# Block 0 of a two-layer conditioned transformer: the scores of a batch in one go instead of two halves, and its first exponential moved to the end of its tick

## The reference

```
h = ln(x) * (1 + scale1) + shift1                     # modulated by cond_1024
q, k, v = split(h @ Wqkv + bqkv)
x = x + attn(q, k, v) @ Wos + bos                     # block p = 0
h = ln(x) * (1 + scale2) + shift2
x = x + attn(h @ Wq + bq, ctx @ Wk + bk, ctx @ Wv + bv) @ Woc + boc   # block p = 1
x = x + gelu(ln_mod(x) @ W1 + b1) @ W2 + b2           # block p = 2
attn: softmax(q k^T / 4) v, per head, over 128 x 128 scores
```

## Time and profile before

| | |
|---|---|
| median of 3 runs | 4214.8 us (4213.77 to 4216.97) |
| the profiled execution | 4216.5 us, of which its span (first to last instruction) 4214.5 us |
| mean granted TensorE clock | 0.996 |
| busy share of the span | PE 96%, PEld 82%, DVE 68%, ACT 65%, POOL 69% |
| blocks p = 0 and 1 | from some 60 to 1190 us, 32 groups of 4 batches |

### The profile page before, as it was taken

One profiled execution on the slowest core, in us unless ns is written; L12 is line 12 of the kernel. 1 busy time (PEld: TensorE's weight loads), 2 busy tenths in 40 slices (PEclk: granted clock), 3 DMA queues, 4 the chain that ended last, 5 costly groups with the idle time before them and its releaser, 6 DMA issues.

```text
span 4214.5 us, 95758 instructions
## 1 busy us (share of the span) xinstructions
PE 4065.3 (96%) x34870; PEld 3476.2 (82%) x34870; DVE 2854.7 (68%) x6066; ACT 2751.0 (65%) x10788; POOL 2905.9 (69%) x2706
## 2 busy tenths in 40 slices
PE   7999999999999999999999999999999999999999
PEld 6777777777779987888888888888888888888998
DVE  7888888888865556565656565777777767665443
ACT  6999999999953335666666666666666666665333
POOL 5777788888767775666566565666666666666776
PEclk9999999999999999999999999999999999999999
DMA  2110011111111122212121212322222222221110
GB/s 82 32 32 32 32 47 39 42 47 47 53 51 47 60 64 76 81 71 81 70 80 71 81 70 95 105 78 91 80 89 86 82 87 81 88 98 56 41 51 31
DMA packets 230900, 276.64 MB, mean 66 GB/s; under 512 B 38044, under 2 KB 160416, under 8 KB 230432
## 3 DMA queue, kind: packets, MB, share of 16 engines
q1 hardware_dynamic: 230364, 270.51, 18.9%
q10 hardware_dynamic: 68, 0.02, 0.0%
HBM read 85.89 MB, written 50.33 MB: 32 GB/s over the span
## 4 chain that ended last, share of the span: by engine, by line
PE 78%; POOL 7%; DVE 7%; ACT 5%; issue 3%; DMA 0%; ACTq 0%; SPq 0%; DVEq 0%; POOLq 0%
PE BANKS L607 18%; PE BANKS L609 16%; PE BANKS L608 16%; PE BANKS L801 7%; PE BANKS L765 6%; PE BANKS L753 6%; PE BANKS L687 3%; ACT PR L904 3%; POOL PR L1234 2%; POOL Z L1277 2%; PE BANKS L823 2%; DVE WL L1095 1%; POOL HL L1244 1%; DVE PT L1058 1%; POOL X L1291 1%
## 5 line engine op out<-in xcount | busy, mean ns | idle before, releaser
L1234 POOL TENSOR_TENSOR PR<-PR,RL 128x512 f32<-128x512 f32 x1024 | 1070.2, 1050 | 656.0 <-DVE RL L1063 654.7
L920 ACT ACTIVATE PR<-BANKS,NM 128x128 f32<-128x128 f32 x2048 | 730.5, 382 | 441.8 <-DVE NM L1109 437.4
L904 ACT ACTIVATE PR<-BANKS,NM 128x128 f32<-128x128 f32 x2048 | 730.8, 412 | 12.6 <-DVE NM L1050 10.5
L607 PE MATMUL BANKS<-HH,WH 128*128 128x512 f32 x1632 | 688.8, 422 | 8.6 <-DVE SN L1123 4.3
L801 PE MATMUL BANKS<-ID,PR 128*128 128x128 f32 x4096 | 624.1, 275 | 61.7 <-DVE OL L1102 26.0
L1109 DVE TENSOR_REDUCE NM<-BANKS 128x8 f32<-128x1024 f32 x256 | 313.3, 1224 | 487.3 <-PE BANKS L765 487.3
L608 PE MATMUL BANKS<-HL,WH 128*128 128x512 f32 x1632 | 642.3, 394 | 0.0
L609 PE MATMUL BANKS<-HH,WL 128*128 128x512 f32 x1632 | 642.0, 393 | 0.0
L801 PEld LDWEIGHTS BANKS<-ID,PR 128*128 128x128 f32 x4096 | 487.4, 140 | 187.3 <-POOL PR L1234 66.7
L904 ACT ACTIVATION_READ_ACCUMULATOR PR<-BANKS,NM 128x1 f32 x2048 | 516.6, 253 | 0.0
L920 ACT ACTIVATION_READ_ACCUMULATOR PR<-BANKS,NM 128x1 f32 x2048 | 452.7, 221 | 0.0
(11 more groups left out here) (132 smaller groups left out, 10733.8 us busy)
## 6 DMA issues: line engine op xcount, KB each, us to landing
SW<-SN SPq DMA_DIRECT2D x1024, 128.0 KB, 2.1
x_scratch<-X SPq DMA_DIRECT2D x80, 512.0 KB, 3.1
X<-x_scratch SPq DMA_DIRECT2D x80, 512.0 KB, 4.0
CX<-in_ctx SPq DMA_DIRECT2D x32, 384.0 KB, 4.2
X<-in_x SPq DMA_DIRECT2D x16, 512.0 KB, 3.9
out<-X SPq DMA_DIRECT2D x16, 512.0 KB, 2.9
CX<-in_ctx SPq DMA_DIRECT2D x32, 128.0 KB, 4.1
STG<-in_L_xcond_W SPq DMA_DIRECT2D x4, 512.0 KB, 5.2
```

The source lines that it names most:

```text
L607: e.matmul(o, lh, rh, start=first and i == 0, stop=False)
L904: made = e.activation(pr[:, r], bank[:, r], ACT.Exp, bias=nm[:, h:h + 1], accum_out=RL[npr(t)[0]][:, h:h + 1])
L920: made = e.activation(pr[:, r], bank[:, r], ACT.Exp, bias=nm[:, h:h + 1], accum_out=RL[npr(t)[0]][:, h:h + 1])
L1234: e.tensor_tensor(p3, p3, RL[npr(t)[0]][:, :].unsqueeze(2).broadcast_to([128, 4, 128]), ALU.mult).then_inc(s_nrm, 1)
```

## The change

The scores of a batch become one stage in tick 0, all four row groups in turn inside the loop (24 matmuls), waiting for tile 3 of the batch before. Both maxima move to tick 0 too. The exponentials become a function that is called twice in a tick: tiles 1 to 3 where they were, tile 0 behind copies, hf and gelu. (On `s_s0` each batch still counts 2.)

```diff
             for b in range(G):
                 tb = tg + 4 * b
+                at["scores0", tb].append(Batch(p, g, b))
                 for h in range(2):
-                    at["scores0", tb + 2 * h - 2].append(Half(2 * (4 * (NG * p + g) + b) + h, p, g, b, h))
-                    at["max0", tb + 2 * h - 1].append(Half(2 * (4 * (NG * p + g) + b) + h, p, g, b, h))
+                    at["max0", tb].append(Half(2 * (4 * (NG * p + g) + b) + h, p, g, b, h))
...
-                    q.wait_ge(s_exp, 4 * (4 * ga + x.b) + 2 * x.h - 2)
+                    q.wait_ge(s_exp, 4 * (4 * ga + x.b))
                     for c in range(2):
                         for k, (qt, kt) in enumerate(((AH, KBH), (AH, KBL), (AL, KBH))):
-                            for r in (2 * x.h, 2 * x.h + 1):
+                            for r in range(4):
...
-                    made.then_inc(s_s0, 1)
+                    made.then_inc(s_s0, 2)
...
+            def exponentials(tiles):
+                for t in tiles:
+                    q.wait_ge(s_nm0, t.n // 2 + 1)
+                    q.wait_ge(s_t, t.n - NP0 + 1)
+                    q.wait_ge(s_nrm, t.n - NP0 + 1)
...
+                    made.then_inc(s_exp, 1)
...
-                for t in at["exp0", tick]:
...
+                exponentials([t for t in at["exp0", tick] if t.u])
...
+                exponentials([t for t in at["exp0", tick] if not t.u])
```

More of the change, by code:

```diff
@@ L871, in _ @@
                     e.dma_start(CROWB[r + 1:r + 2, 64 * i:64 * i + 64], a[key][128:CD].unsqueeze(0)).then_inc(s_crows, 16)
+            def exponentials(tiles):
[3 more added lines that the diff above has]
+                    q.wait_ge(s_nrm, t.n - NP0 + 1)
+                    bank, pr, nm = PS[t.u], PR[npr(t)[0]], NM0[t.n // 2 % 3][:, 4 * (t.n % 2):4 * (t.n % 2) + 4]
+                    for h in range(4):
+                        r = slice(128 * h, 128 * h + 128)
+                        made = e.activation(pr[:, r], bank[:, r], ACT.Exp, bias=nm[:, h:h + 1], accum_out=RL[npr(t)[0]][:, h:h + 1])
+                    made.then_inc(s_exp, 1)
             for tick in ticks:
```

## The result

The changed kernel takes 4502.6 us (median of 4 runs, 4500.6 to 4504.0) against 4215.9 for the kernel before: a ratio of 1.068, with a 95% interval of 1.067 to 1.069. It is 287 us slower. The prediction was 4513.

A forecast was written before the change was run, and what follows sets the result against it. No single engine but the fixed order of four loaded engines was taken to bound p = 0 and 1. Span 4214.5 + 117 + 86 + 95 = 4512, plus 2.0 outside is 4514.5, so 4513 us for the median; range 4290 to 4630.

The forecast's parts named there:

- The forecast case: Whole kernel: slower through VectorE's tick 0 plus a clock loss, 4513 us for the median; chance 0.48.
- Part 1, four row groups: TensorE's scores: four row groups overlap as pairs do, 24 matmuls cost 0.91 us, saving 0.91 us of TensorE per batch.
- Part 2, the walk: Blocks p = 0 and 1: VectorE's tick 0 waits for scores, lengthening groups by 7.3 and 5.4 us, +117 and +86 us.
- Part 3: ScalarE: placing tile 0's exponentials last in their tick costs nothing, put at 0.
- Part 4, the clock: TensorE in p = 0 and 1: longer idle gaps lower its clock about 1.5 times a group, +95 us, bounds 0 and 210.
- The clock holds: Rival, TensorE's clock: the walk is right and the clock does not fall, 4418 us; chance 0.22.
- The bare ScalarE loop: Rival, ScalarE: only its loop binds, batches of 8.1 to 9.5 us, 4230 to 4330 us in all; chance 0.15.
- Two pairs at a time: Rival, TensorE's scores: four row groups run as two pairs, +116 us on the forecast, 4630 us; chance 0.06.
- TensorE's order as the bound: Rival, TensorE: the saved 0.91 us shortens every batch while the maxima hide, at best 4125 us, half 4170; chance 0.06.

The follow-up runs named there:

- e5: The changed kernel with each pv0 computed three times into the same bank, filling TensorE's idle time with useless work: 4451.1 us.
- e3: The changed kernel with the exponentials of tile 0 back in their old place in the tick: 4502.9 us.
- e7: The kernel before with only the exponentials of tile 0 moved to the end of their tick: 4215.9 us.
- e8: The kernel before, its two halves of scores where they were, but both maxima in tick 0: 4423.4 us.
- e6: The changed kernel with the scores of tick 0 issued as two halves one after the other, two row groups at a time: 4493.1 us.
- e2: The changed kernel with both maxima of tick 0 issued on VectorE behind the copy, the reciprocal and q_low or k_low: 4417.4 us.
- e9: The changed kernel with half 0's maximum first in tick 0 and half 1's in tick 1 behind low0: 4431.0 us.
- e10: The kernel before with only the maximum of half 1 moved behind low0 within tick 1: 4256.9 us.
- e12: The kernel before with each pv0 computed twice: 4272.9 us.
- e1: The changed kernel with the maximum of half 1 one tick later on VectorE, in tick 1 instead of tick 0: 4464.6 us.

## Why the prediction was right, by its steps

**The forecast case** was the one that happened: slower, by the chain through VectorE's tick 0, with a loss to the clock on top. Forecast +298 us (4513 less the 4215 of the median), measured +287.

**Part 1, four row groups**: right, 0.91 us, bound for bound. Pairs and quads start together and the next step follows at the same distance (24 matmuls in six steps of four take 0.91 us, as 12 in six steps of two did). The factor of 3.07 that the Trainium skill gives (TensorE: Matmul & The Clock Gate, Part 3) would have meant 1.19 us; the trace shows no such loss.

**Part 2, the walk**: shown. Its batches against e5, where the clock is 1.00, from one start of scores to the next:

| | batch 0 | 1 | 2 | 3 | group |
|---|---|---|---|---|---|
| p = 0, predicted | 10.0 | 9.75 | 11.4 | 11.0 | 42.2 |
| p = 0, e5 | 9.90 | 9.68 | 11.50 | 11.37 | 42.45 |
| p = 1, predicted | 10.6 | 9.4 | 11.1 | 10.9 | 42.0 |
| p = 1, e5 | 10.72 | 10.05 | 11.28 | 11.38 | 43.43 |

For p = 0 the term of 117 us measured (42.45 - 34.87) x 16 = 121. For p = 1 the 86 measured (43.43 - 36.64) x 16 = 109. Two waits are missing from the walk there. In batch 1 of p = 1 "k has six matmuls, so 9.4" let k start behind v_out, as in p = 0. But VectorE merges the context behind v_out, without a pause (GpSimd's split for it had ended at 876.1), and k waits for the merge (VectorE, then TensorE):

```profile
879.12 0.46 DVE L1079 TENSOR_TENSOR V<-BANKS,TB 128x128 f32<-128x128 f32 x2
879.61 0.68 DVE L1015 TENSOR_REDUCE HH<-HL 64x512 fp32r<-64x512 f32 x1
```

```profile
880.39 0.47 PE L709 MATMUL BANKS<-ONES,BK 128*128 128x512 f32 x1 [0.86 <-DVE HH L1015]
```

And "GpSimd's long run of norms and splits then just fits into the longer cycle" does not quite hold: in batch 3 of each group from 430 to 1035 us, p = 0 too, the q projection waits some 0.63 us for GpSimd's split, as here:

```profile
859.60 0.50 PE L607 MATMUL BANKS<-HH,WH 128*128 128x512 f32 x1 [0.62 <-POOL HL L1244]
```

These rows are e5's again. The first fits the 0.65 us that batch 1 of p = 1 took above the walk, the second the 0.4 to 0.5 of batch 3. Both terms together, 203 predicted, are 230 by these rows and 235.7 by the medians (4451.1 - 4215.4).

**Part 3**: 0, as predicted (e3, e7).

**Part 4, the clock**: the mechanism was right, the size was not. 95 predicted, 51.5 measured (4502.6 - 4451.1). Behind the gap of 3.52 us before 625.52 the changed kernel has

```profile
625.00:630.00 5.00, 4.48 (x25) 4.51 (x26) 3.60 (x11) 3.49 (x20) 3.06 (x4) 0.66 0.00 0
```

so the falls came. From 551 to 700 us the granted clock went down to 0.50 eight times, each time for less than 4 us, and each began in one of TensorE's gaps of 2.2 to 3.5 us or less than 1 us behind it. The time spent there is near what I had: (1 - 0.90) x 2 x 1395 us is some 280 us at the lower level (nearly all of it in these blocks), over 31 groups 9 us each, where I had 7.5. But it came in more and shorter stretches, 2 to 3 a group instead of 1.5 of five us; the bounds of the prediction from its rows were 2.4 and 14 us, and no row of before gave the 3.4 to 7.

What I mis-sized is what a microsecond at the lower level costs. I let 2.2 of 5 us be lost; 51.5 over 32 groups is 1.6 a group, 0.9 of 5. The batches show where: with a fall in them those of p = 0 take 10.64, 10.85, 12.67 and 11.76 us (batches 0 to 3), against 9.90, 9.68, 11.50 and 11.37 in e5, so a fall costs 0.4 us in batch 3, 0.7 in batch 0 and 1.2 in the others. Right behind a gap TensorE is ahead of low0 again (v and tile 2's transposes are early): in batches 2 and 3 of the regular groups with a fall low0 ends 6.36 and 7.25 to 7.35 us after the scores, in e5 6.35 and 7.25. So what of the slow stretch lies ahead of low0 costs nothing or 0.1 us. I allowed 10 of 105 us for that, and it was about half.

The two misses cancel in part, +33 and -44. So that 4502.6 came so close to 4513 is partly luck.

**The rivals.** "The clock holds" is out (0.90 in the blocks), and its time of 4418 would have been 4451 (its sum as written, 4213 + 203, is 4416; the 4418 goes from the median). The bare ScalarE loop is out: with it the scores would wait for the last exponential, and in 400 to 1000 us they never do; a batch of the regular groups takes 9.65 to 12.7 us, not 8.1 to 9.5. (Its groups of 36.5 to 38 us would have given some 4240 to 4290, not 4230 to 4330.) Two pairs at a time is out by the x4 rows. TensorE's order as the bound is out: it needed the two maxima to delay low0 by less than 0.91 us, and in batch 3 low0 ended 7.35 us after the scores instead of 4.28, which is 3.1 later. The walk's own 7.2 made that 2.9, where the prediction says 2.0. In its first paragraph it also gives ScalarE the highest share in both groups; by the unions of rows 1 TensorE's 32.78 is above ScalarE's 32.34 in p = 0.

**How the experiments split 287 us**: 208 for the maxima in tick 0 alone (e8, with its own clock loss in it), 70 more for half 0's scores in tick 0 as well (e6 less e8), 9.5 between e6 and the changed kernel, which the regular groups don't show, 0 for the exponentials. The clock's share within e8 and e6 was not measured.

## What to carry to other kernels

Where four engines run fixed orders at 80 to 90% load, walk the ring of waits once with start-to-start distances, and for every instruction that gets a later input write down what stands behind it in its own queue: the 0.91 us saved on TensorE were real, but no engine could take the scores sooner, and each new place for the maxima (e2, e9, e10) only moved the stall along the ring. If TensorE comes to idle between bursts by as much as here (gaps of 1.8 to 3.5 us), add a term for its clock, but charge the lower level only for the part of the slow stretch that is on the chain. Repeating matmuls in the gap (e5) separates the two, if the batches without a fall keep their length by it; where TensorE's work is on the chain (e12) it only costs.

## What the runs showed that I had not expected

- Two halves of scores on different row groups, issued one after the other, overlap by half: the first matmuls of half 1 start at 601.31 with the fourth step of half 0, and 24 matmuls take 1.26 us instead of 1.82 (e6).
- The clock fell as much with shorter gaps: in e1 TensorE's longest in a group of p = 0 were 1.8 and 2.4 us, one fall came about half a microsecond behind the 1.80, and the clock of the whole span was 0.964, the same as with gaps of 2.9 and 3.5 us in the changed kernel. The gap of 1.85 us before 1176.46 in the kernel before had hinted at it.
- Some 112 us of useless matmuls made a kernel 26 us faster, and the same ones made the kernel before 57 us slower.
